# Attention and a gated feed-forward part planned together: products with V kept in stock, seven probability tiles, single score units

## The reference, cut to what matters

```python
xn = layernorm(x)                                # x: 2 x 8192 x 1024
latent = xn @ Wc_down                            # 512 wide
q = latent @ Wq_up                               # 16 heads of 64
k, v = split(latent @ Wkv_up)                    # one k and one v for all heads
att = softmax(causal(q k^T / 8))
s = (att v) @ Wc_proj
g = silu(ffn(xn))                                # silu(xn Wg) * (xn Wu), times Wd; 3072 hidden
out = x + s * g
```

## Time and profile before

| | |
|---|---|
| median of 3 runs | 1488.38 us (1488.12 to 1488.52) |
| the profiled execution | 1486.96 us |
| span of its slowest core, core 0 | 1485.4 us (cores: 1476.2 to 1485.4) |
| PE, PEld, ACT, DVE, POOL busy | 92%, 54%, 81%, 46%, 13% |
| mean DMA traffic | 111 GB/s |

### The profile page before, as it was taken

How to read it: one execution, slowest core, us unless ns; L and a number is a source line. 1 busy time by engine, 2 the same in 40 slices (tenths; PEclk the granted TensorE clock), 3 DMA queues, 4 the chain that set the end, 5 groups by cost and what they waited for, 6 DMA issues and landing times.

```text
span 1485.4 us, 44737 instructions; the slowest of 8 cores (1476.2 to 1485.4 us)
## 1 busy us (share of the span) xinstructions
PE 1366.6 (92%) x17929; PEld 799.7 (54%) x18064; DVE 690.0 (46%) x1321; ACT 1198.4 (81%) x1254; POOL 198.6 (13%) x352
## 2 busy tenths in 40 slices
PE   2689998899999899999998999999999899999998
PEld 2555555555555556555555555555555555555553
DVE  3678765677574535535334134333332323333325
ACT  3576676777879797997987997998999799998971
POOL 3322122222212212001001012000000112000000
PEclk9899999999999999999999999999999999999999
DMA  9825555476848463421221332421223043212113
GB/s 235 149 86 134 138 111 152 126 184 141 212 124 243 106 198 95 129 73 68 91 79 38 108 104 91 128 73 44 73 73 119 23 140 122 72 64 82 58 45 106
DMA packets 64762, 164.68 MB, mean 111 GB/s; under 512 B 7728, under 2 KB 15152, under 8 KB 64560
## 3 DMA queue, kind: packets, MB, share of 16 engines
q1 hardware_dynamic: 52272, 131.26, 27.3%
q0 software_dynamic: 12288, 30.54, 11.2%
HBM read 151.42 MB, written 33.55 MB: 125 GB/s over the span
## 4 chain that ended last, share of the span: by engine, by line
PE 74%; ACT 8%; issue 7%; DVE 5%; DMA 4%; POOL 1%; DVEq 0%; ACTq 0%; SPq 0%; POOLq 0%
PE ps L230 73%; ACT p_sb L957 6%; DMA h_sb<-wkv 2%; PE ps L241 2%; DVE bnd L570 1%; ACT p_dg L957 1%; POOL p_dg L965 1%; DMA wgub<-wgu_sb 1%; DMA xt<-xb 1%; DVE g_sb L708 1%; DMA wdr<-wd 1%; DVE xnT L473 0%; DVE xn L413 0%; ACT xnT L470 0%; ACT xn L409 0%
## 5 line engine op out<-in xcount | busy, mean ns | idle before, releaser
L957 ACT ACTIVATE p_sb<-ps,nbias 128x1024 bf16<-128x1024 f32 x1024 | 1064.0, 1124 | 150.3 <-PE ps L230 149.7
L230 PEld LDWEIGHTS ps<-vaug,p_sb 128*128 128x128 bf16 x8192 | 310.1, 97 | 190.9 <-issue 154.5
L230 PE MATMUL ps<-vaug,p_sb 128*128 128x65 bf16 x8192 | 386.7, 194 | 24.6 <-DVE p_sb L965 10.1
L230 PE MATMUL ps<-own_f,wgu_sb 128*128 128x512 bf16 x1536 | 393.3, 380 | 7.2 <-DVE g_sb L708 2.1
L230 PE MATMUL ps<-qT,kT 64*128 64x256 bf16 (+1 forms) x4352 | 331.5, 270 | 15.1 <-DVE xnT L473 4.1
L230 PEld LDWEIGHTS ps<-qT,kT 64*128 64x128 bf16 x4352 | 165.0, 94 | 218.7 <-issue 197.5
L230 PE MATMUL ps<-wdr,h_sb 128*128 128x512 bf16 x696 | 182.8, 380 | 5.6 <-DMA wdr<-wd 0.4
L230 PEld LDWEIGHTS ps<-own_f,wgu_sb 128*128 128x128 bf16 x1536 | 126.2, 97 | 109.5 <-issue 11.8
L708 DVE COPY g_sb<-ps 128x512 f32<-128x512 f32 x96 | 66.2, 690 | 190.7 <-PE ps L230 190.1
L710 ACT ACTIVATE t_sb<-g_sb 128x512 f32<-128x512 f32 x96 | 60.8, 634 | 55.3 <-DVE g_sb L708 51.3
L230 PEld LDWEIGHTS ps<-wdr,h_sb 128*128 128x128 bf16 x768 | 62.5, 98 | 50.5 <-issue 4.1
(11 more groups left out here) (100 smaller groups left out, 996.2 us busy)
## 6 DMA issues: line engine op xcount, KB each, us to landing
wgu_sb<-wgub SPq DMA_DIRECT2D x72, 512.0 KB, 3.4
xt<-xb SPq DMA_DIRECT2D x57, 512.0 KB, 6.0
wdr<-wdb SPq DMA_DIRECT2D x72, 256.0 KB, 3.7
wgu_sb<-wgu POOLq DMA_DIRECT2D x24, 512.0 KB, 7.7
wgub<-wgu_sb SPq DMA_DIRECT2D x24, 512.0 KB, 7.0
out<-acc_sb POOLq DMA_DIRECT2D x28, 256.0 KB, 3.5
wdr<-wd POOLq DMA_DIRECT2D x24, 256.0 KB, 8.4
wdb<-wdr SPq DMA_DIRECT2D x24, 256.0 KB, 8.1
```

The source lines that it names most:

```text
L230: return p.op("tensor", lambda e: e.matmul(out, lhsT, rhs, start=start, stop=stop, skip_group_check=shared), waits, "pe" if tok else None, ...
L957: ex = A(cost, lambda en, dst=dst, src=src, bias=bias: en.activation(dst, src, AF.Exp, bias=bias, scale=0.125), [mm, p_prior(u)[1], bias_t ...
```

## The change

`PR` goes from 6 to 7 and `DR` from 11 to 10; a tile of either ring has the same size. The planner sums the costs of what it has given TensorE (`pe_work`). A flag `single` is set when the FFN is done, or when there are two score buffers and the exps still to come (985 ns each) plus 40 us exceed what TensorE has left (1195 us less `pe_work`, plus 100 ns for each unit to come). With it, one unit may be scored alone. `kept_av` counts the products that are ready in a row from the next one on, up to the last unit of a pass. A product has its old place ahead of the other work only if five or more are ready, or if the unit where the count ended is the last of its pass; otherwise it is offered behind `work` and the FFN.

```diff
--- before.py
+++ after.py
@@ -34,13 +34,16 @@
 NBLK = NG // 4
 XR = 4
 WR = 3
-DR = 11
-PR = 6
+DR = 10
+PR = 7
 NPASS = 4
 LB = NG - 4
 PRO = 4
 SCALE3 = 0.25 * SIG ** 3
 INF = 1e18
+PE_WORK = 1195e3
+SPARE = 40e3
+KEEP = 5
 
 
 class Tok:
@@ -65,6 +68,7 @@
         self.items = {}
         self.sems = {}
         self.only_pe = {}
+        self.pe_work = 0.0
         self.T = {"tensor": 0.0, "vector": 0.0, "scalar": 0.0, "gpsimd": 0.0, "sync": 0.0}
         self.dma_t = {"sync": 0.0, "gpsimd": 0.0}
 
@@ -83,6 +87,8 @@
             t = max(t, w.t)
         t += cost
         self.T[engine] = t
+        if engine == "tensor":
+            self.pe_work += cost
         if dma:
             self.dma_t[engine] = max(self.dma_t[engine], t) + dma / self.RATE[engine]
             t = self.dma_t[engine] + 4500.0
@@ -1164,23 +1170,31 @@
                     give(5, bufs[i][1])
                     del bufs[i]
                     nbuf = 2
+
+            single = lazy.done or nbuf == 2 and (NU - nu) * 985.0 + SPARE > PE_WORK - p.pe_work + (NU - nu) * 100.0
             if nu < NU:
                 n = 0
                 at = 0.0
                 while n < nbuf and nu + n < NU and unit_t(nu + n) < INF:
                     tn = max(unit_t(nu + n), ready(*bufs[n][1]))
-                    if n >= 2 and tn > t0:
+                    if n >= (1 if single else 2) and tn > t0:
                         break
                     at = max(at, tn)
                     n += 1
-                if n >= 2 or n and (nu + n == NU or units[nu + n][0] > units[nu][0]):
+                if n >= 2 or n and (single or nu + n == NU or units[nu + n][0] > units[nu][0]):
                     offer(at, ("s", n))
-            if na < nu:
+
+            kept_av = 0
+            while na + kept_av < nu and av_t(na + kept_av) <= t0 and not units[na + kept_av][5]:
+                kept_av += 1
+            if na < nu and (kept_av >= KEEP or units[min(na + kept_av, NU - 1)][5]):
                 offer(av_t(na), ("v", na))
             for w in work:
                 offer(w.at(), ("w", w))
             if not lazy.done:
                 offer(lazy.at(), ("w", lazy))
+            if na < nu:
+                offer(av_t(na), ("v", na))
             if nu == NU and nbuf:
                 nbuf = 0
                 for sb, fr in bufs:

```

## The result

The changed kernel takes 0.9638 of the time of the kernel before (95% interval 0.961 to 0.9666): 1434.5 us against 1488.4, 54 us or 3.6% less. I had forecast 1455 (2.2% less) with a range from 1438; the direction was right, the gain was more than half as large again, and the time lies just under the range. A later repetition gave 0.9639 (0.9618 to 0.9661).

What follows compares the result with a forecast made beforehand. TensorE's whole program was taken as the bound: 1485.4 - 42 - 5 + 6 + 4 = 1448 us, plus 4 for meeting chains gives span 1452, plus 3.0 gives 1455 us; range 1438 to 1485.

Steps and rivals of the forecast that it cites:

- Which chain ends last: TensorE's whole program ends last, the chain of exps 38 us earlier; shortening TensorE's program counts until the exps end last.
- Step 1: Products held back until five are ready, so waits for exps, masks and normalisation shrink: 42 us saved, bounds 15 and 52.
- step 4: Seven tiles: with a full stock a product must precede the next pair; 9 us on the chain of exps.
- Step 2: Stocked products run while the FFN's only bank is being evicted: 5 us of TensorE idle time saved, bounds 0 and 12.
- Step 3: TensorE reaches its scores earlier and waits there for the buffer an exp holds: 6 us added, bounds 0 and 25.
- Rival A: TensorE's waits move from products to score buffers, since exps set the pace from 1050 on: 1477 us, chance 0.18.
- The hold: Full ring of seven tiles delays the next pair's scores until a product runs: 9 us on the chain of exps.
- the 4 us added for chains that meet: At the end both chains finish within 3 us, and TensorE meets gaps its filler could fill before: 4 us added.
- Step 5: Units scored alone: 0.19 us per further batch, 4 us on TensorE, bounds 0 and 12; 5 us given to ScalarE.
- Step 6: Ten tiles of down weights instead of eleven: 0 us, or 5 us if other work no longer covers the idle time.
- Rival D: Fewer short stops also recover granted clock, up to 8 us: time 1447 us; chance 0.62 together with the forecast.

Runs made afterwards that it cites:

- age alone: Kernel before with seven and ten tiles, products in their old place only from 1 us after their exp or mask: 0.9963, 1483 us.

## Why the prediction was right or wrong

*Which chain ends last.* Right. TensorE's whole program set the end, and what was taken off it came off the time: 57 us less lost on core 5 against 52 us less span, with 11 batches more.

*Step 1, products in stock, 42 us.* Mis-sized. Lost time before products fell by 27 us. The masks did what was said (20 us forecast as waits before, of which 14 to go; 24 us by start distances fell to 11). The rest did not: 28 of 31 us were to go, and 27 fell to 12. The sum also took all 11.7 us of waits for an exp as standing before products, where the earlier trace rows has 6.6. And 22 waits for a fresh exp remain (9.9 us, 6.4 of them before products): a stock that fills gaps is emptied by them, and the next product is young again. Of the 1088 products of units in the changed kernel 382 start with five or more in stock, and 118 with one. The prediction took the stock to be full always in this step and emptied by bank waits in step 4; both can't hold.

*Step 2, filler, 5 us.* This is the step that failed. It was 19 us by the start distances of other work, and by the experiments the filling is most of the whole, the waits before products included: age alone gives 15 us of 63 against the kernel with the same tiles, and a longer eviction goes nearly in full into the time. The error was one of reading. I took the releaser's name for the cause: a wait that an exp ends was booked as a late exp. But a wait before a product mostly comes about when neither scores nor other work are ready, so the question is why there was no other work, and the answer, one bank for all of it, stands in no row of a wait on that exp. The bound of 12 us came from idle time before gate and up matmuls, where a bank wait shows only if the FFN is what ends it.

*Step 3, waits that come instead, +6 us.* Wrong sign, and in the sum the largest miss, 17 us: lost time before scores fell by 11 us. Rival A, which made this its case, didn't happen.

*Step 4 and the chain of exps.* The hold, if it is what acts at six, cost nothing that can be seen at five. The chain ended 35 us earlier on core 5, not 9. The forecast had counted only the products' waits before 700 us as reaching it. My reading is that each stop of TensorE also delays the next scores, and that the tanh of a gate keeps exps waiting in ScalarE's queue; its waits fell as well (11.3 to 3.1 us). That late stretch had less room for scores, as I said (15.4 to 11.4), but I had left the tanh out. So the 4 us added for chains that meet weren't due either: 18 us of down matmuls and projection still follow the last exp.

*Step 5, singles.* Right in size: 0.19 us each, 11 more batches, few us.

*Step 6, ten tiles.* The tile is hardly missed (1.0 us of waits), but the two ring sizes alone cost 9 us, above my bound.

*The sum.* Steps 1, 2 and 3 were -42, -5 and +6, together -41; measured by start distances -27, -19 and -11, together -57. The total missed by 16 us; the 4 us for chains that meet make it 20. That it missed by no more is partly luck: step 1 was 15 us too large and step 2 14 us too small, and these cancel. A range that had taken the upper bound of step 1 and of step 2 together (1485.4 - 52 - 12 + 4, plus 3: 1428) would have held the time, with step 3 at nothing. The range was said to take the upper gain bounds and yet began at 1438; no sum on record gives that end.

*What stays open.* How much of the gain is exactly filler and how much age can't be split further by these runs, since a larger stock also makes products older. The doses (nearly none, three, four, five products: 6, 22, 43, 54 us under the kernel before; the four with six tiles) say that the length of the stock is what pays. Orders that differ slightly vary by several us for reasons that were not found.

## What to carry to other kernels

Ask of each wait on the bottleneck engine not only what ended it but why nothing else was ready; doubling one suspected cost, here an eviction, tells much of it in one run. Small pieces of work that need no scarce resource are worth most when kept back for the moments in which everything else waits for that resource. Here a stock of five went well with a ring of seven and one of six did not, which fits a bound of the ring less what the producer takes at once, two. The stock also had to be released early where a chain of dependent steps begins.

## What was not expected of the hardware

Nothing in the chip's behaviour was new; three numbers are worth keeping. Products with V keep their pitch when many stand together: the 48 that begin at 1403.27 are followed by the next matmul at 1404.73, 30 ns each, and so they are cheap filler. The Trainium skill (TensorE: Matmul & The Clock Gate, Back-to-back issue gap) gives about 81 ns for a matmul of 128 columns in a stream in which each has a weight load. The trace differs: such matmuls start 56 ns apart in the median (1580 pairs of the changed kernel, core 5). A change of TensorE from 512-column matmuls to scores on half of the rows and back costs 0.19 us a batch (96 ns there, and some 93 in the 202 ns from the last scores to what follows), and the 356 further batches agree. And TensorE with 29 us of lost time in 1384, after the first 100 us, kept a mean granted clock of 0.992 to 0.998 on the cores of that kernel (no third buffer), against 0.989 to 0.994 in the kernel before with 105 us lost and 0.991 to 0.996 in the changed one with 48. Rival D's bonus is there at most in sign; the ranges overlap, and it is a fraction of a per cent.
